# A four-stage graph network and mixture-of-experts kernel: one round of its pipeline written in another order

## What is computed

```python
def _L0_gnn_ref(h, adj, W, a):          # h is the layernormed x
    Wh = jnp.einsum('bnd,de->bne', h, W)
    e = (Wh @ a1)[:, :, None] + (Wh @ a2)[:, None, :]
    e = jnp.where(adj > 0, jax.nn.leaky_relu(e, 0.2), NEG_INF)
    out = jnp.einsum('bij,bjd->bid', jax.nn.softmax(e, axis=-1), Wh)
    return jax.nn.elu(out)

def _L0_ffn_ref(features, ...):         # E = 6, TOP_K = 2
    rh = jax.nn.relu(features @ router_w1 + router_b1)
    expert_logits = jax.nn.softmax(rh @ router_w2 + router_b2, axis=-1)
    top_w, top_i = jax.lax.top_k(expert_logits, TOP_K)
    routing_weights = jax.nn.softmax(top_w, axis=-1)
    h1 = jax.nn.relu(jnp.einsum('bsd,edh->bseh', features, expert_w1) + expert_b1)
    h2 = jax.nn.relu(jnp.einsum('bseh,ehf->bsef', h1, expert_w2) + expert_b2)
    expert_out = jnp.einsum('bsef,efo->bseo', h2, expert_w3) + expert_b3
    return sum over the two chosen experts of routing_weights * expert_out

x = x + _L0_gnn_ref(_layernorm(x), adj, ...)
x = x + _L0_ffn_ref(_layernorm(x), ...)
x = x + _L1_gnn_ref(_layernorm(x), adj, ...)   # the same attention, other weights
x = x + _L1_ffn_ref(_layernorm(x), ...)        # router on the mean over nodes, two of eight experts, gelu, layernorm
```

## Time and profile before

| | us |
|---|---|
| median of 3 runs | 721.52 (720.93 to 721.79) |
| the profiled execution | 721.59 |
| its span, first to last instruction | 719.8 |

### The profile page before, as it was taken

The page is one execution under the profiler, slowest core; times in us unless marked ns, Lnnn a source line. Parts: engine busy times, 40 slices in busy tenths (PEclk is TensorE's granted clock), DMA queues, the critical chain, the costliest instruction groups (busy, mean ns, idle before and its releaser), DMA issues. The chain is left out here.

```text
span 719.8 us, 15213 instructions
## 1 busy us (share of the span) xinstructions
PE 593.0 (82%) x3969; PEld 481.7 (67%) x4001; DVE 455.4 (63%) x1632; ACT 393.0 (55%) x914; POOL 290.4 (40%) x507
## 2 busy tenths in 40 slices
PE   3468899889898898988989889788522999999993
PEld 2345577667676676767667667566411999999993
DVE  3365668887887877878778787674423144444445
ACT  1234566666665666656666666655421466566552
POOL 4312214553444534535355354343421044444444
PEclk9999999999999999999999999999955899999998
DMA  7404304224042140440412402202001644444422
GB/s 164 111 0 134 112 23 132 67 68 133 3 131 87 45 132 10 122 123 9 132 38 94 132 0 89 87 3 91 0 0 40 185 130 141 142 129 144 144 60 58
DMA packets 74597, 61.98 MB, mean 86 GB/s; under 512 B 7772, under 2 KB 62268, under 8 KB 74562
## 3 DMA queue, kind: packets, MB, share of 16 engines
q1 hardware_dynamic: 61344, 56.14, 26.0%
q10 hardware_dynamic: 13218, 5.42, 2.9%
HBM read 57.13 MB, written 4.41 MB: 85 GB/s over the span
## 5 line engine op out<-in xcount | busy, mean ns | idle before, releaser
L1324 PE MATMUL bank<-w,h2w 128*128 128x128 f32 x768 | 105.4, 281 | 26.1 <-DVE h2w L1008 26.1
L1324 PEld LDWEIGHTS bank<-w,h2w 128*128 128x128 f32 x768 | 96.0, 194 | 31.9 <-DVE h2w L1008 29.8
L798 ACT ACTIVATE h<-bank,b 128x512 f32<-128x512 f32 x96 | 66.0, 688 | 92.7 <-PE bank L1311 92.7
L1311 PE MATMUL bank<-h,w 128*128 128x512 f32 x192 | 104.9, 630 | 1.0 <-ACT h L803 1.0
L803 ACT ACTIVATE h<-bank,b 128x512 f32<-128x512 f32 x96 | 65.7, 684 | 29.3 <-PE bank L1305 28.8
L1008 DVE TENSOR_TENSOR h2w<-h,wide_w 128x512 f32<-128x512 f32 x96 | 70.7, 736 | 16.8 <-ACT h L798 16.8
L1303 PE MATMUL bank<-xnTh,w1h 128*128 128x512 f32 x96 | 69.4, 723 | 0.0
L347 POOL TENSOR_TENSOR x<-x,at_prT 128x512 f32 (+1 forms) x16 | 23.7, 1481 | 80.3 <-DVE at_prT L328 80.3
L101 POOL TENSOR_TENSOR at_var_eps<-at_mean_var,eps 128x4 f32<-128x4 f32 x32 | 13.2, 412 | 102.9 <-DVE at_mean_var L94 102.9
L335 POOL TENSOR_TENSOR at_src<-at_wh,zero 128x8 bf16<-128x8 f32 x32 | 9.8, 306 | 84.0 <-DVE at_wh L303 84.0
L251 PEld LDWEIGHTS wide<-at_wh,at_prT 128*128 128x128 f32 x256 | 33.6, 204 | 13.7 <-ACT at_prT L287 5.2
(11 more groups left out here) (234 smaller groups left out, 1511.5 us busy)
## 6 DMA issues: line engine op xcount, KB each, us to landing
wide_w<-w_scratch SPq DMA_DIRECT2D x96, 256.0 KB, 4.5
mask<-in_L_ffn_W SPq DMA_DIRECT2D x128, 128.0 KB, 2.1
x<-in_x SPq DMA_DIRECT2D x16, 256.0 KB, 6.0
xin<-in_x SPq DMA_DIRECT2D x16, 256.0 KB, 6.1
adj_in<-in_adj SPq DMA_DIRECT2D x16, 256.0 KB, 6.3
out<-at_pr ACTq DMA_DIRECT2D x8, 256.0 KB, 2.7
out<-at_prT ACTq DMA_DIRECT2D x8, 256.0 KB, 2.7
W<-in_L_ffn_W SPq DMA_DIRECT2D x2, 512.0 KB
```

The costliest lines, as they stand in the source:

```text
L798: a.activation(h2[:, e % 2, :], b_h2[:, :], ACT.Relu, bias=b2[:, e:e + 1]).then_inc(h2_ready, 1)
L1311: pe.matmul(b_h2[:, :], w2[:, e, :], h1[:, e % 2, :], start=True, stop=True).then_inc(l2_done, 1)
L1324: last = pe.matmul(b_out[:, s], h2w[:, e % 2, s], w3[:, e, :], start=False, stop=(e == E0 - 1), skip_group_check=True)
```

## The change

Only the order in which four engines' rounds are written changes, on three of them: GpSimd, ScalarE and VectorE. TensorE and SyncE keep theirs, and no operation is added or taken out.

- The route's measure and root move from the start of round i, for group i+1, to the end of the round before, for the same group; VectorE applies the route's norm directly behind at0's `attn_dve_wh`.
- VectorE: at1's `attn_dve_y` goes behind the route's application; `weigh` of expert 1 ahead of at1's elu and at0's max; `weigh` of expert 2 ahead of at1's wh and the mask, so that pool's measure follows the mask; at0's elu and `weigh` of expert 4 ahead of at1's max, the route's measure and `route_weights`.
- ScalarE: the route's first exponential goes ahead of relu2 of expert 3; at0's elu passes go ahead of relu1 of expert 5.
- GpSimd: the route's root goes behind at0's residual.

```diff
--- before.py
+++ after.py
@@ -710,8 +710,6 @@
             def body(i, i0):
                 if live("attn0", i0):
                     attn_pool_split(at0, p, zero, i + 2)
-                if live("route", i0):
-                    norm_root(rn, p, eps, minus_half, i + 1, rn["xn_ready"])
                 if live("attn1", i0):
                     norm_root(at1["norm"], p, eps, minus_half, i - 1, at1["wh_ready"])
                 if live("attn1", i0, -1) and not last(i0):
@@ -725,15 +723,16 @@
                     p.tensor_copy(rstd3[:, bass.ds(g * GG, GG)], pn["rstd"][:, :])
                     p.wait_ge(pn["shift_step"], 2 * g + 2)
                     p.tensor_copy(shift3[:, bass.ds(g * GG, GG)], pn["shift"][:, :])
-                    if last(i0):
-                        return
-                    settle(p, const_ready)
-                    need(p, p_xnT_done, g)
-                    norm_apply_pool(pn, p, p_xn[:, :], x[:, cols(g)], const_ready, g)
+                    if not last(i0):
+                        settle(p, const_ready)
+                        need(p, p_xnT_done, g)
+                        norm_apply_pool(pn, p, p_xn[:, :], x[:, cols(g)], const_ready, g)
                 if live("norm0", i0):
                     norm_root(at0["norm"], p, eps, minus_half, i + 3, at0["wh_ready"])
                 if live("attn0", i0):
                     attn_pool_residual(at0, p, x, x[:, cols(i + 2)], const_ready, i + 2)
+                if live("route", i0, 1):
+                    norm_root(rn, p, eps, minus_half, i + 2, rn["xn_ready"])
                 if i0 == -LEAD["attn0"]:
                     later_constants()
 
@@ -861,28 +860,29 @@
                 if attn0:
                     attn_act_exp(at0, a, i + 2)
 
+                if route:
+                    a.wait_ge(route_step, ROUTE * (i + 1) + 2)
+                    a.activation(pe0[:, :, :], lgd[:, :, :], ACT.Exp).then_inc(pe0_ready, 1)
                 if run:
                     relu2(n + 3, 3)
                 if attn0:
                     attn_act_prT(at0, a, i + 2)
                 if run:
                     relu1(n + 4, 4)
-                if route:
-                    a.wait_ge(route_step, ROUTE * (i + 1) + 2)
-                    a.activation(pe0[:, :, :], lgd[:, :, :], ACT.Exp).then_inc(pe0_ready, 1)
                 if attn1:
                     attn_act_rows(at1, a, i - 1)
 
                 if run:
                     relu2(n + 4, 4)
+                if attn0:
+                    attn_act_elu(at0, a, i + 2)
+                if run:
                     relu1(n + 5, 5)
                 if attn1:
                     attn_act_z(at1, a, i - 1)
                 if route:
                     a.wait_ge(route_step, ROUTE * (i + 1) + 7)
                     a.activation(pq[:, :, :], pd[:, :, :], ACT.Exp).then_inc(pq_ready, 1)
-                if attn0:
-                    attn_act_elu(at0, a, i + 2)
                 if pool:
                     pooled(i - 2)
 
@@ -1106,14 +1106,12 @@
                 if attn0:
                     attn_dve_wh(at0, v, i + 2)
                 if route:
-                    measure(rn, i + 1, at0["x_ready"], i + 2)
+                    need(v, r_xnT_done, i + 1)
+                    norm_apply(rn, v, buf_tile(r_xn), x_tile(i + 1), i + 1)
+                if live("route", i0, -1):
+                    weight_low(i)
                 if live("attn1", i0, -1):
                     attn_dve_y(at1, v, i - 2)
-                if live("route", i0, -1):
-                    weight_low(i)
-                if route:
-                    need(v, r_xnT_done, i + 1)
-                    norm_apply(rn, v, buf_tile(r_xn), x_tile(i + 1), i + 1)
                 if live("experts", i0, -1):
                     v.wait_ge(l3_done, i * E0)
                     need(v, at1["x_ready"], i - 2)
@@ -1121,7 +1119,6 @@
                         .then_inc(x_experts_ready, 1)
                 if attn1:
                     measure(at1["norm"], i - 1, x_experts_ready, i, lambda t: xe[:, (i0 + 1) % 2, t * P:(t + 1) * P])
-
                 if run:
                     weigh(n, i, 0)
                 if route:
@@ -1130,6 +1127,9 @@
                     v.wait_ge(xnTh_ready, g + 1)
                     v.tensor_tensor(xnTl[:, par, :], b_misc[:, :], xnTh[:, par, :].bitcast(F32),
                                     ALU.subtract).then_inc(xnTl_ready, 1)
+
+                if run:
+                    weigh(n + 1, i, 1)
                 if live("attn1", i0, -1):
                     attn_dve_elu(at1, v, i - 2)
                     if last(i0):
@@ -1138,18 +1138,15 @@
                             .then_inc(at1["x_ready"], 1)
                 if attn0:
                     attn_dve_max(at0, v, i + 2)
-
-                if run:
-                    weigh(n + 1, i, 1)
                 if live("norm0", i0):
                     measure(at0["norm"], i + 3, x_loaded, 16 * (i + 3) + 16)
+                if run:
+                    weigh(n + 2, i, 2)
                 if attn1:
                     attn_dve_wh(at1, v, i - 1)
                 if live("norm0", i0):
                     make_mask(i + 3, (i0 + 1) % 2)
 
-                if run:
-                    weigh(n + 2, i, 2)
                 if pool:
                     measure(pn, i - 2, at1["x_ready"], i - 1)
                     if last(i0):
@@ -1167,15 +1164,16 @@
                     attn_dve_y(at0, v, i + 2)
                 if run:
                     weigh(n + 3, i, 3)
+                if attn0:
+                    attn_dve_elu(at0, v, i + 2)
+                if run:
+                    weigh(n + 4, i, 4)
                 if attn1:
                     attn_dve_max(at1, v, i - 1)
+                if live("route", i0, 1):
+                    measure(rn, i + 2, at0["x_ready"], i + 3)
                 if route:
                     route_weights(i + 1)
-                if attn0:
-                    attn_dve_elu(at0, v, i + 2)
-                if run:
-                    weigh(n + 4, i, 4)
-                if route:
                     weight_rows(i + 1)
                 if run:
                     weigh(n + 5, i, 5)
```

More of the change, by code:

```diff
@@ L1169, in body @@
                     weigh(n + 3, i, 3)
-                if attn1:
-                    attn_dve_max(at1, v, i - 1)
-                if route:
-                    route_weights(i + 1)
                 if attn0:
@@ L1177, in body @@
                     weigh(n + 4, i, 4)
+                if attn1:
+                    attn_dve_max(at1, v, i - 1)
+                if live("route", i0, 1):
+                    measure(rn, i + 2, at0["x_ready"], i + 3)
                 if route:
+                    route_weights(i + 1)
                     weight_rows(i + 1)
```

## The result

| | kernel before | changed kernel |
|---|---|---|
| median, us | 721.22 (720.25 to 721.79, 4 runs) | 766.17 (765.06 to 767.70, 4 runs) |
| ratio to before, 95% interval | 1 | 1.0626 (1.0602 to 1.0651) |
| span of the profiled execution, us | 719.8 | 765.2 |
| mean granted clock of TensorE | 0.948 | 0.915 |

The change costs 45 us, 6.3%. The forecast was 753 with a range up to 766: right in direction and place, 13 us short in size, and the measured time is 0.2 outside the range.

A forecast was written before the change was run, and what follows sets the result against it. TensorE, with waits for `weigh` of expert 3 and the route's rows, was taken as the bound. 13 rounds at 31.1 for 29.2 (+25.0), start +7.1 and round 14 -0.5 gave +31.6: 753 us, range 737 to 766.

The forecast's parts named there:

- The walk of the chain from R: Steps from a round's start (R) on TensorE through at0's aggregate to the weights' transpose at 25.9, next round at 30.3.
- r_xn, h2w of expert 3: TensorE's waits for the route's normalised rows (0.79) and for `weigh` of expert 3 (1.97) in a round: both go.
- the 1.44 wait: VectorE's wait for the route's first exponential, queued behind relu2 of expert 3 on ScalarE: goes.
- the two 0.8 stalls of `prob` and `over`: VectorE operations held beside GpSimd's full-width p_xn passes: both stalls go, with 0.2 to spare.
- The rival of weights in time: At `weights_transpose`: no TensorE wait over 0.3, a round of 25.4 to 26.2, about 676 to 685 us; 3%.
- The second form of the lighter rival: GpSimd's residual goes ahead of at1's max and the clock costs nothing: round 30.3, up to 742; whole rival 20%.
- the clock term: Slower TensorE clock after the wait at `weights_transpose`, in nearly all rounds: 0.8 a round, between 0.4 and 1.2.
- the falls of the kernel before: Six clock drops behind the 1.97 wait ahead of layer3 of expert 3: 1.2 each, 7 us of 720.
- The heavier rival: at_y and the chain slip by 0.7 and every clock fall costs 1.2: round 32.2, 767 us; 12%.
- a slipped rank: On VectorE, `route_rank` lacks its 0.2 to spare, one operation falls behind p_xn, the chain slips by 0.7.
- The start: Rounds -1 and 0: transpose of round -1 later by 5.8, round 0 longer by 1.3, together +7.1.
- Round 14: No at0 work and no measure there, weights ready about when they were: -0.5.

The follow-up runs named there:

- experiment 5: Changed kernel with at1's max ahead of `weigh` of expert 4 and, on ScalarE, at1's z copy ahead of relu1 of expert 5: 754.66 us.
- experiment 1: Changed kernel with `route_weights` directly behind `weigh` of expert 3, ahead of at0's elu, and its exponential placed earlier: 670.87 us.
- experiment 3: Changed kernel with 24 small matmuls, results unread, on TensorE ahead of each weights' transpose: 742.48 us.
- experiment 2: Changed kernel with the route's measure behind `route_weights` and `weight_rows`: 741.32 us.
- experiment 7: Kernel before with ten small matmuls, results unread, in the wait ahead of layer3 of expert 3: 714.40 us.
- experiment 4: Changed kernel with at1's max ahead of `weigh` of expert 4 on VectorE: 769.21 us.

## Why the prediction was wrong in size, step by step

**Right.** The place and the mechanism: the wait at `weights_transpose`, 4.66 where it said 4.6. The walk of the chain from R, each as forecast and then measured: aggregate 17.0 and 17.3; at0's elu starts 19.85 and 20.07; residual 20.8 to 22.3 and 21.02 to 22.49; at1's max ends 23.55 and 23.76; the measure 24.8 and 25.01; the transpose 25.9 and 25.98. That GpSimd goes first in the middle of two two-tensor operations of VectorE, so that max's first operation takes 1.75: read right from a small operation of the earlier trace rows, and shown by experiment 5, where turning the order round gave the time back. What goes away: r_xn, h2w of expert 3, the 1.44 wait, the two 0.8 stalls of `prob` and `over`. The rival of weights in time named what experiment 1 is, and gave 676 to 685 for 671. That the clock would fall in nearly all rounds: it fell in all 13. The second form of the lighter rival (the residual goes first and the clock costs nothing) gave 742, and experiment 3, where this was so, 742.5. The measure's share was 1.25 a round in the walk and 1.23 in experiment 2.

**Wrong: the clock term, 0.8 taken between 0.4 and 1.2.** It measured 1.8, more than the upper end. The rest of the round was right: 30.3 in the prediction, 30.33 in experiment 3, whose 13 rounds have no slow stretch. With it the changed kernel's round was 32.17, so the term was 1.84. The shown round says the same within 0.1: 25.98 from R to the transpose leaves 6.19 of 32.17 from the transpose to the next R, 1.77 over the 4.42 of full clock. Behind a 3.4 us stretch at 1.2 GHz it was 6.00 (341.62 to 347.62), a price of 1.58; behind 6.8 us 6.75 (373.60 to 380.35), 2.33. The 1.0 that was missing, 13 times, is 13.5 us of the 13.8 by which the profiled execution missed. Two things failed in the step. First, the length of a slow stretch was taken as fixed, since all before had been 3.4 us; in 7 of the 13 rounds it was 6.8. Second, the upper end was the price of the falls of the kernel before, 1.2, and even a stretch of 3.4 us cost 1.58 here. That a part would pass inside the wait was right for the long stretch at 372.6 (1.0 of 6.8 us) and not for the short one at 341.9 (nothing). In the kernel before, the 3.4 us cost 1.2 in part because the slow transposes there took in the wait of 0.23 for wgt of the earlier trace rows; the remaining 0.15 is not explained. From the timeline of the kernel before, 309 to 318 us, where the weights' transpose comes 3.07 after layer3 of expert 3 started (309.57) instead of 2.27 (280.87 to 283.14), and then 4.83 ahead of the next R instead of 4.42:

```profile
312.64 0.42 PE L1330 MATMUL wide<-ident,wgt 128*88 128x128 f32 x1
312.85 1.38 PE L1311 MATMUL bank<-h,w 128*128 128x512 f32 x2
```

and from that of the changed kernel, 341 to 348 us, where the slow stretch lies on the wide matmuls of layer2 and layer1 with no wait to take in (1.10 and 0.80 at full clock):

```profile
341.82 1.99 PE L1309 MATMUL bank<-h,w 128*128 128x512 f32 x2
342.83 1.42 PE L1301 MATMUL bank<-xnTh,w1h 128*128 128x512 f32 x1
```

The heavier rival had the right time (32.2 a round, 767) but in part for the wrong reason, by luck: 0.7 of it was to come from a slipped rank, which did not happen (25.98), and 1.2 from the clock, which cost 1.8 by itself.

**The rule that would have left the term out.** The falls of the changed kernel cost 13 x 1.84 = 24 us, 3% of its span, and experiment 3 gave 23.7 us back by removing them. The Trainium skill ("TensorE: Matmul & The Clock Gate", the part on what is actually happening in the clock gate) says: "For modeling, the ramp penalty is <1% of a typical kernel span; don't fit to a specific cold count." The sentence stands with the slow matmuls at a kernel's start; it was the prediction that read it as a rule for falls behind waits. Read so, the kernel before agrees with it at about 1% (7.0 us of 721, experiment 7), and the changed one does not; the measurement decides. The sum for this change, which puts a wait of 4.66 us into every round, had to have the term.

**Small terms.** The start cost 5.7 where 7.1 was said: the transpose of round -1 moved by 6.7 instead of 5.8, but round 0, which was to grow by 1.3, shrank by 1.0 (59.16 to 84.78, for 52.46 to 79.10). Round 14 grew by 0.1 instead of losing 0.5, and the end by 0.7. In sum: 13 rounds at 32.17 instead of 31.1, +13.9 (13.5 of it the clock), -1.4, +0.6 and +0.7 make 13.8, and the spans differ by 45.4 where 31.6 was said. Two sums of the prediction do not come out of its own rows, and neither is in the forecast: a round without the waits is 28.7 - 0.79 - 1.97 - 0.23 = 25.7, not 25.4, and "13 times 3 to 3.8 less" than 721.5 is 672 to 683, not 676 to 685. The 1.04 that it gives as GpSimd's sum alone is the row of p_xn, another operation of the same width.

**Open.** The half clock of the last section, from 557 to 608 us in the changed kernel, is in all these kernels (some 41 to 51 us of it), and no experiment changed it on purpose. The waits for at1's probabilities that are left in experiment 1 (6.6 us in its rounds) were not tried either. Why the slow stretches come in turns of 3.4 and 6.8, and why the waits of 1.97 brought the clock down in six of twelve rounds and not in the others, is not explained.

## What to carry to other kernels

When a step is moved, look at what stands behind it on the same engine and who is waiting there: here two full-width operations, a third that GpSimd's sum held up, and 1.25 us of statistics that wait for that sum stood ahead of four tiny operations, 1.1 us in all, that TensorE needed, and giving these the first idle gap turned a 6% loss into a 7% gain (671 us). Price a long wait of TensorE by more than its length: a single wait of 4.66 cost 1.6 to 2.3 beyond itself, while 1.97 cost 1.2 in half of its rounds, and where the wait stayed, small matmuls in it were a gain (24 us and 7 us). What a slow stretch costs lies in the work behind the wait, so a price taken from one kernel does not hold for another wait.

## What the runs showed of the hardware

- The length of the slow stretch is not fixed. After waits of 1.97 and 3.43 us it was 3.4 us at 1.2 GHz; after 3.94 (experiment 5) 3.4 in ten rounds and 6.8 in one; after 4.66, and after 5.05 in experiment 4, it was 3.4 and 6.8 in turns, from round to round. Waits of 1.97 brought the clock down in six of twelve rounds, waits of 4.66 in every one. With TensorE kept busy by small bf16 matmuls, no stretch was left in the rounds (experiments 3 and 7).
- VectorE and GpSimd excluded each other by whole full-width operations with two inputs, in the order of arrival, and one that waited went before the next of the other engine's queue: 0.69 for max alone becomes 1.75 behind a residual that itself waited for `weigh`; 0.12 and 0.34 us between the two arrivals decided the order in experiments 4 and 5. The reduction with one input ran beside GpSimd at its full 0.69. This is not so for every operation of GpSimd: its root on 128x4 (L104, 1.01 us from 353.67 in the changed kernel) did not hold `weigh` at 353.97, which took its usual 0.68.
